# The first routed expert of a mixture in two runs of groups: eight places wide, then five places wide

## The reference, cut to what matters

```
gate_scores = softmax(logits of the batch)            # four experts
topk_w, topk_i = top_k(gate_scores, 2); topk_w = topk_w / (topk_w.sum() + 1e-8)
for e in range(4):
    h = gelu(x @ ew1[e] + eb1[e]);  y = h @ ew2[e] + eb2[e]      # 256 -> 1024 -> 256
    out = out + w_be[:, e] * mask[e] * y                          # w is 0 where e was not chosen
shared = gelu(x @ sw1 + sb1) @ sw2 + sb2
return x + out + shared
```

## Time and profile before

| | |
|---|---|
| median of 3 runs | 647.63 us (647.61 to 648.51) |
| span of the profiled execution | 646.8 us; it lies 0.8 us below the median of the runs |
| PE busy | 636.0 us, 98% |
| DVE, ACT, POOL busy | 412.4, 317.4, 255.3 us |
| matmuls | 5704 |
| granted TensorE clock, mean | 0.996 of full speed |

### The profile page before, as it was taken

One profiled execution on the slowest core, in us unless ns is written; L12 is line 12 of the kernel. 1 busy time (PEld: TensorE's weight loads), 2 busy tenths in 40 slices (PEclk: granted clock), 3 DMA queues, 4 the chain that ended last, 5 costly groups with the idle time before them and its releaser, 6 DMA issues.

```text
span 646.8 us, 16422 instructions
## 1 busy us (share of the span) xinstructions
PE 636.0 (98%) x5704; PEld 540.5 (84%) x5704; DVE 412.4 (64%) x951; ACT 317.4 (49%) x599; POOL 255.3 (39%) x504
## 2 busy tenths in 40 slices
PE   9999999999999999999999999999999999999995
PEld 6999888888888888888788888888888888888895
DVE  4998987665575666668767644544455785555555
ACT  5655454434444344444547544444446664444453
POOL 1657775445455454533325333033303422332100
PEclk9999999999999999999999999999999999999998
DMA  6520210000000000000002100000001320000006
GB/s 252 196 81 24 64 51 2 0 1 1 0 0 0 0 0 0 1 1 2 0 2 83 50 0 0 0 0 0 0 0 33 98 83 0 0 0 0 0 1 261
DMA packets 8023, 20.77 MB, mean 32 GB/s; under 512 B 816, under 2 KB 1584, under 8 KB 7472
## 3 DMA queue, kind: packets, MB, share of 16 engines
q1 hardware_dynamic: 7696, 19.63, 8.8%
q10 hardware_dynamic: 288, 0.64, 0.3%
HBM read 16.07 MB, written 4.19 MB: 31 GB/s over the span
## 4 chain that ended last, share of the span: by engine, by line
PE 95%; DVE 3%; issue 1%; ACT 0%; POOL 0%; ACTq 0%; DVEq 0%; POOLq 0%
PE zy L1016 57%; PE hp L1016 38%; DVE d_t L666 0%; DVE h_b L669 0%; DVE w_buf L646 0%; DVE d_t L663 0%; DVE acc L961 0%; DVE h_b L653 0%; ACT y_all L623 0%; DVE g_lo L640 0%; DVE first L673 0%; DVE shared_buf L712 0%; ACT uc L487 0%; DVE h_r L654 0%; DVE h_b L657 0%
## 5 line engine op out<-in xcount | busy, mean ns | idle before, releaser
L640 DVE TENSOR_TENSOR g_lo<-g_f,g_hi 128x512 fp32r<-128x512 f32 (+2 forms) x167 | 121.8, 730 | 154.0 <-ACT g_hi L508 148.6
L1016 PE MATMUL zy<-g_hi,w_buf 128*128 128x512 f32 (+2 forms) x704 | 183.1, 382 | 0.4 <-issue 0.4
L508 ACT ACTIVATE g_hi<-g_f 128x512 fp32r<-128x512 f32 (+2 forms) x176 | 107.6, 612 | 150.6 <-PE zy L1016 150.3
L501 ACT ACTIVATE g_f<-hp,first 128x512 f32<-128x512 f32 (+3 forms) x180 | 120.2, 668 | 118.5 <-PE hp L1016 114.4
L1016 PE MATMUL hp<-shared_buf,w_buf 128*128 (+1 forms) x672 | 169.1, 386 | 0.0
L1016 PEld LDWEIGHTS hp<-shared_buf,w_buf 128*128 128x128 f32 x672 | 126.0, 188 | 24.9 <-issue 0.3
L1016 PEld LDWEIGHTS zy<-g_hi,w_buf 128*128 128x128 f32 x704 | 126.1, 188 | 23.6 <-ACT g_hi L508 0.6
L1016 PE MATMUL zy<-g_lo,w_buf 128*128 128x512 f32 (+2 forms) x352 | 105.1, 380 | 0.0
L1016 PE MATMUL hp<-x_hl,w_buf 128*128 (+2 forms) x432 | 104.7, 378 | 0.2 <-DVE w_buf L646 0.2
L1016 PEld LDWEIGHTS zy<-h_b,y_all 128*128 128x128 bf16 x2976 | 90.7, 98 | 15.5 <-issue 13.1
L1016 PE MATMUL zy<-h_b,y_all 128*128 128x64 bf16 x2976 | 98.4, 193 | 0.8 <-DVE h_b L669 0.6
(11 more groups left out here) (148 smaller groups left out, 488.6 us busy)
## 6 DMA issues: line engine op xcount, KB each, us to landing
stage<-in_w_exp SPq DMA_DIRECT2D x40, 256.0 KB, 2.8
out_y<-acc SPq DMA_DIRECT2D x2, 1376.0 KB, 4.9
acc<-in_x SPq DMA_DIRECT2D x1, 2048.0 KB, 9.1
acc<-in_x SPq DMA_DIRECT2D x1, 1536.0 KB, 9.2
out_y<-acc SPq DMA_DIRECT2D x1, 1344.0 KB, 5.4
acc<-in_w SPq DMA_DIRECT2D x1, 512.0 KB, 4.5
acc<-in_x SPq DMA_DIRECT2D x2, 256.0 KB, 6.1
acc<-in_w ACTq DMA_DIRECT2D x1, 512.0 KB, 5.4
```

The costliest lines, as they stand in the source:

```text
L501: act.activation(raw_of(j, n, keep), hp[j % 2][:, 0:n], ACT.Gelu_apprx_tanh, bias=par[:, S_B1 + e * NCH + j:S_B1 + e * NCH + j + 1]).then_ ...
L508: act.activation(chunk_of(j, n, keep)[0], raw_of(j, n, keep), ACT.Copy).then_inc(ghi_done, 1)
L640: dve.tensor_tensor(lo, raw_of(j, n, keep), hi.bitcast(F32), ALU.subtract).then_inc(glo_done, 1)
L1016: return pe.matmul(out_, lhsT=lhsT, rhs=rhs, start=start, stop=stop, skip_group_check=True)
```

## The change

Expert 0 gets two loops instead of one, q = 0 with groups of 8 places (512 columns) and q = 1 with groups of 5 places (320 columns), both with the same weights. Experts 3, 1, 2 become q = 2, 3, 4. For n0 batches in expert 0 there are as many groups in all as are needed when at least one has five places, and one, two or three of them have five, as few as hold n0. By the thresholds of `GROUP_AT`, n0 = 53 gives six groups of eight and one of five. Nothing is loaded or split for q = 1 (`LOADS`), and its loop body is a new one on every engine.

`gate_slots` changes: three counts stand for expert 0 (`cnt`), and the starts come from a table. Batches of expert 0 beyond the full groups are placed by steps of five.

```
-SPLIT = 2
-PER = [SLOTS, SLOTS, WIDE, LAST]
+RUN_OF = [0, 0, 3, 1, 2]
+WEIGHTS_OF = [1, 1, 2, 3, 4]
+LOADS = [2, None, 3, 4, None]
+NQ = len(RUN_OF)
+END = NQ - 1
+SHORT = 5
+PER = [SLOTS, SHORT, SLOTS, WIDE, LAST]
...
+LESS = SLOTS - SHORT
+FEWEST = 3
+GROUP_AT = [over([SLOTS * j - LESS * a for j in range(FEWEST + a // 3, B)], NC) for a in (1, 2, 3)]
...
-            for q in range(E):
+            for q in range(NQ):
...
-                    if q < E - 1:
+                    if q < END and LOADS[q] is None:
+                        for j in range(NCH):
+                            gelu_chunk(r + NS, j, e, n)
+                    elif q < END:
...
 # gate_slots
-                link(dve.tensor_copy(ngr, gp[:, 2 * E:3 * E]))
-                link(dve.tensor_tensor(cmp8[:], ngr.unsqueeze(2).to_broadcast([P, E, SLOTS]), ...GROUP_AT..., ALU.is_gt))
-                link(dve.tensor_reduce(ngr, cmp8[:], AX_X, ALU.add))
-                link(dve.tensor_scalar(ngr, ngr, 1.0, None, ALU.max))
+                dve.tensor_copy(cnt[:, 0:3], gp[:, 2 * E:2 * E + 1].to_broadcast([P, 3]))
+                link(dve.tensor_copy(cnt[:, 3:NCNT], gp[:, 2 * E + 1:3 * E]))
+                link(dve.tensor_tensor(cmp_c, cnt.unsqueeze(2).to_broadcast([P, NCNT, NC]), ...GROUP_AT..., ALU.is_gt))
+                dve.memset(ngr[:, NCNT:NCNT + 1], 1.0)
+                link(dve.tensor_reduce(ngr[:, 0:NCNT], cmp_c, AX_X, ALU.add))
...
+                dve.tensor_scalar(more, iota[:, 1:1 + NJ], full[0:B], 0.0, ALU.subtract, ALU.max)
-                dve.tensor_tensor(cut3, ...)
+                link(dve.tensor_tensor(cut3, ...))
+                link(dve.scalar_tensor_tensor(out=jump[:, 0], in0=more, scalar=-float(LESS), in1=jump[:, 0],
+                                              op0=ALU.mult, op1=ALU.add))
...
+                dve.tensor_scalar(past, before[:, 0:1], full[0:B], 0.0, ALU.subtract, ALU.max)
                 dve.tensor_scalar(cut, cut, 2.0 * MANY, WIDE - 2.0 * MANY, ALU.mult, ALU.add)
+                link(dve.tensor_scalar(gslot, start_f[0:B, 0:E], float(WIDE), float(MANY), ALU.mult, ALU.add))
                 link(dve.tensor_tensor(before, before, con[0:B, C_BY:C_BY + E], ALU.mult))
-                link(dve.tensor_scalar(gslot, start_f[0:B, 0:E], float(WIDE), float(MANY), ALU.mult, ALU.add))
+                dve.scalar_tensor_tensor(out=before[:, 0:1], in0=past, scalar=float(LESS), in1=before[:, 0:1],
+                                         op0=ALU.mult, op1=ALU.add)
...
 # the list of batches by slot, on PE
-                    mm(lists[0:32, 0:NSLOT], con[0:B, C_BIDX:C_BIDX + 32], pick, True, True)
+                    mm(lists[0:1, 0:NSLOT], con[0:B, C_BIDX:C_BIDX + 1], pick, True, True)
```

More of the change, by code:

```diff
@@ L84 @@
 C_BIDX = C_IOTA + NSLOT
-C_EIGHTS = C_BIDX + 32
-C_TIE = C_EIGHTS + E * SLOTS
+C_EIGHTS = C_BIDX + 1
+C_TIE = C_EIGHTS + NCNT * NC
 C_CUM = C_TIE + E * E
-C_JUMP = C_CUM + (E + 1) * E
-C_BY = C_JUMP + E * (SLOTS - 1)
+C_JUMP = C_CUM + (NQ + 1) * (NCNT + 1)
+C_BY = C_JUMP + E * NJ
 C_CUT = C_BY + E
@@ L180, in cond_resid_kernel @@
         den = gs[0:B, 50:51]
-        ngr = gs[:, 51:55]
-        start_f = gs[:, 55:60]
+        cnt = gs[:, 65:65 + NCNT]
+        ngr = gs[:, 72:72 + NCNT + 1]
+        start_f = gs[:, 51:51 + NQ + 1]
+        full = start_f[:, COL_OF[1]:COL_OF[1] + 1]
+        more = gs[0:B, 22:22 + NJ]
+        past = gs[0:B, 57:58]
         gslot = gs[0:B, 60:64]
@@ L243, in raw_of, with group_bounds @@
             return g_f[:, j % 2, 0:n]
-        def group_bounds(eng, which=range(E + 1)):
+        def group_bounds(eng, which=range(1, NQ + 1)):
             eng.wait_ge(starts_done, 1)
-            return [eng.value_load(starts[0:1, e:e + 1], min_val=0, max_val=MAXG) for e in which]
+            return [eng.value_load(starts[0:1, COL_OF[q]:COL_OF[q] + 1], min_val=0, max_val=MAXG) for q in which]
         def y_bank(r):
@@ new lines, in gate_slots @@
+                link(dve.tensor_reduce(start_f, cum, AX_X, ALU.add))
+                dve.tensor_copy(starts, start_f).then_inc(starts_done, 1)
+                pos = gp[0:B, E:2 * E]
+                jump = con[0:B, C_JUMP:C_JUMP + E * NJ].rearrange("p (e s) -> p e s", s=NJ)
+                dve.tensor_scalar(more, iota[:, 1:1 + NJ], full[0:B], 0.0, ALU.subtract, ALU.max)
+                link(dve.tensor_tensor(cut3, pos[:, SPLIT_E:SPLIT_E + 1].to_broadcast([B, len(CUT_AT)]),
+                                       con[0:B, C_CUT:C_CUT + len(CUT_AT)], ALU.is_equal))
@@ L811, in gate_slots @@
+                link(dve.scalar_tensor_tensor(out=jump[:, 0], in0=more, scalar=-float(LESS), in1=jump[:, 0],
+                                              op0=ALU.mult, op1=ALU.add))
+                link(dve.tensor_tensor(cmp_j, pos.unsqueeze(2).to_broadcast([B, E, NJ]), jump, ALU.is_ge))
                 dve.tensor_reduce(cut, cut3, AX_X, ALU.add)
-                link(dve.tensor_reduce(before, cmp8[0:B, :, 0:SLOTS - 1], AX_X, ALU.add))
+                link(dve.tensor_reduce(before, cmp_j, AX_X, ALU.add))
@@ L937, in slots_at @@
             def slots_at(q, per, i):
[L939 removed]
+                cuts = [min((3 if q == END else 2) * c, per) for c in range(NCH)]
                 return list(range(cuts[i], cuts[i + 1])) if i + 1 < len(cuts) else []
             def finish_last(r, q, bs):
[L944 removed]
+                e, n = RUN_OF[q], TOKS[RUN_OF[q]]
                 dve.wait_ge(add_done, (r + 1) * WIDE + 1)
@@ L975, in _ @@
             last_bs = []
-            for q in range(E):
-                e = ORDER[q + 1]
+            for q in range(NQ):
                 n = COLS[q]
-                keep = q == E - 1
+                keep = q == END
                 with dve.Fori(sv[q], sv[q + 1]) as r:
@@ L1279, in _ @@
             mm(lists[:, NSLOT:2 * NSLOT], ones_f[0:B], pick_w, True, True).then_inc(weight_mm, 1)
-            for q in range(E):
+            for q in range(NQ):
                 n = COLS[q]
-                w = w_of(q + 1)
+                i = WEIGHTS_OF[q]
+                w = w_of(i)
                 with pe.Fori(sv[q], sv[q + 1]) as r:
```

137 lines of the change are left out of this document (70 added, 67 removed).

## The result

The kernel after takes 641.36 us (median of 4 runs, 640.70 to 641.67) against 647.62 us before: the ratio is 0.9896, with a 95% interval of 0.9885 to 0.9908, so 6.7 us faster. (The two medians themselves are 6.3 us apart; the interval reaches from 6.0 to 7.4 us, and single runs of one kernel differ by up to 1.5 us.) 640.0 us was predicted, with a range of 639.2 to 642.0. On two later occasions the same kernel gave 0.9884 (0.9869 to 0.9899) and 0.9896 (0.9879 to 0.9912).

The account below looks back on a forecast made before the run. PE's back-to-back matmuls were taken as the bound. 646.8 us of span - 7.68 for columns + 0.05 for loads = 639.2, plus 0.8 from span to median gives 640.0 us; range 639.2 to 642.0.

Parts of the forecast that it names:

- the first rival: Narrow group: DVE becomes the bound, with 0.18 us of slack at chunk 2; price 0.3 to 1.6 us, chance 0.09.
- the first two rivals: DVE bounding the narrow group (up to 1.6 us, chance 0.09) and gate_slots' jump operation losing the port (0.9 us, 0.07).
- The columns: Group 6 narrowed from 512 to 320 columns: 96 matmuls at 146.7 instead of 226.7 ns, a gain of 7.68 us.
- The new structure at nothing: Step between loops: one more loop with its branch on PE, ACT, POOL and DVE costs 0, at most 0.2 us.
- The five loads: DVE's five register loads, moved between groups 5 and 6, hold it 1.61 us; costed 0.05 us, bounds nothing to 1.6.
- gate_slots at nothing: gate_slots' 28 instructions instead of 23 cost 0, since the jump operation precedes POOL's subtraction at 318.63 and later waits absorb the rest.
- From span to median: Whole kernel: the median of the runs lies 0.8 us above the profiled span, taking 639.2 to 640.0 us.
- DVE late: Narrow group: DVE's work or loads delay PE, slack 0.18 us at chunk 2; 640.3 to 641.6 us, chance 0.09.
- the port lost: gate_slots: the jump operation begins after POOL's at 318.63 and waits; PE loses about 0.9 us at the list, 640.9; chance 0.07.
- Weight loads: Narrow group: weight loads of 188 ns bound the matmuls, gain only 3.7 us, so 643.9 us; chance 0.02.
- more groups: Expert 0 gets 54 to 56 batches, so five groups of eight and three of five; 646.4 us, chance 0.01.
- the clock: Group 6 at 1.2 GHz: 25.6 us in place of 21.8, 651.4 us; chance 0.03 with any other slower loss.

Follow-up runs that it names:

- two wide runs: Kernel after with both loops of expert 0 eight places (512 columns) wide, so new loops and gate but no narrow matmul; 648.23 us, ratio 0.9999 to the kernel before.
- ten loads: Kernel after with all ten register loads of the last group behind the loop q = 0, ahead of the narrow group; 641.70 us, ratio 0.9901 to the kernel before.
- the jump operation late: Kernel after with two more linked three-column DVE operations ahead of the jump operation in gate_slots; 641.96 us, ratio 0.9907 to the kernel before.

## Why the prediction was right, point by point

The time lay in the stated range, and the mechanism is the one that was forecast. But the median was 1.4 us above the forecast and outside the 639.6 to 640.5 us that had a chance of 0.74 (640.69 and 641.28 on the later occasions). It fell among the prices of the first rival, 640.3 to 641.6 us, which did not occur, and the upper end of the range had been made for the first two rivals; to that extent it is luck that the range held. Of the 1.4 us, 0.5 lies at the last store (below), which the prediction has no term for. The other 0.9 us is not much more than the difference between medians of one and the same kernel: 647.6 to 648.3 us before, 640.7 to 641.4 after.

*The columns.* 146.7 ns a matmul was forecast and 146.7 measured. The saving was forecast as 7.68 us. The stretch shows 7.61, because a chunk in which widths alternate takes 2.26 us and not 2.24; over the whole of PE's path it is 615.25 - 607.63 = 7.62 us. That the weight load, shown as 188 ns, doesn't bound was right down to 256 columns (120.0 ns).

*The new structure at nothing* was right: 0.9999 with two wide runs, and the same path on PE within 0.1 us.

*The five loads.* 0.05 us was forecast, 0 found. The slack (0.18 us counted, 1.10 - 0.87 = 0.23 by ten loads) and the place (chunk 2) were right. Their own price was somewhat too high: 1.3 us for the first five and 1.1 for five more, against 1.61. I had taken DVE's whole time from one operation to the next for the loads.

*gate_slots at nothing* was right, with the jump operation at 318.31 and POOL at 318.48. The count of the delayed path gave 0.9 us, the experiment 0.8. What the prediction put down as the rule of who waits was too narrow: "those with one or with PSUM didn't" is wrong for one operand, as L849 (0.61 us) and the added operation (to 319.36) show. The same 64x4 operation took 0.15 us in the kernel with the jump operation late, where POOL was idle at its turn. The wait did no harm in the kernel after, since L849 stood where DVE was going to wait anyway.

*From span to median.* The sum itself comes out the same either way (647.63 - 7.63 = 640.0 us). But the 0.8 us between them are not what lies around a span: that is 1.76 us, and the profiled execution was one of the longer ones, by its first matmuls.

*What is missing.* The three comparisons gave 6.7, 7.5 and 6.7 us, against 7.6 on PE's path. In all traces with a narrow group the last store took 5.5 us or more, and in the three of the kernel before and of two wide runs 5.0. From the last addition to the end of the span it is 5.5 us before (641.30 to 646.8) and 6.0 after (633.50 to 639.5). This 0.5 us is at the very end, where nothing hides it, and 7.6 - 0.5 = 7.1 us lies within all three intervals (7.6 us alone would lie just outside the first). The traces say the same without the noise of the beginning: from the first 256-column matmul of x to the end of the span it is 630.3, 630.2 and 630.2 us in the two traces of the kernel before and in that with two wide runs, and 623.1, 623.2 and 623.2 in the three of the kernel after. That 0.5 us is lost behind the last addition is measured; the rest of the difference between the comparisons, 6.7 to 7.5 us, is within their noise. Why the last store took longer is open: it isn't the program (two wide runs have the same one, but for widths), and it isn't simply the distance of the two stores.

The rivals: DVE late and the port lost are both real mechanisms, absent here by 0.2 us each. Weight loads, more groups and the clock were not seen (14 groups, spacing by columns, clock 1.00, that is 2.4 GHz, in the narrow group). The granted clock fell to 0.50, 1.2 GHz, when PE's last matmul was over (631.8 us; window 636 to 640 us). The stretch of 256 columns that the prediction called just as dense had PE busy for 8.98 of 9.42 us; the narrow group, with all of its 15.07 us, is the better evidence.

## What to carry to other kernels

Where matmuls run back to back and no other engine is near, padding columns cost their full time, and a narrower copy of the loop for the last group cost PE nothing here; measure the spacing of a width in the same trace at a neighbouring width, not at the duration shown for a weight load. What narrows a stage shortens the cover of every fixed cost beside it: register loads and a chain of tiny operations were 0.2 us away from being paid. And bring a profiled span to a median only with that run's own time, or compare ratios.

## What the runs showed of the hardware

- The spacing of back-to-back fp32r matmuls with a weight load each was 120.0, 146.7, 193.3 and 226.7 ns at 256, 320, 430 and 512 columns, though the loads are shown with 188 ns. 506 columns took the time of 512: a chunk of expert 1 in the kernel before lasted 2.72 us (540.92 to 543.64), as one of expert 0.
- A DVE operation with one operand in SBUF can be held by POOL too: 64x4 took 0.61 us and ended 0.02 us behind POOL's subtraction, while a 64x1 beside it (318.99) took 0.20 us. The Trainium skill, "SBUF — State Buffer", section "SBUF: two separate sides", names DVE operations in a 2-port mode beside those with two inputs; the trace doesn't show in which mode an operation ran.
- Two executions of one program differed by 1.2 us within their first 16 us and hardly afterwards. The first 14 matmuls of PE made it: 4.27 and 5.45 us, by how long they kept a pace of 0.43 us each before going about twice as fast.
- Loading five batch numbers into registers held DVE for about 1.3 us, five more for 1.10 us.
- The last store of 1376 KB took 5.0, 5.5 or 6.0 us, and it repeated: 5.0 in both traces of the kernel before, 5.5 in all three of the kernel after.
